# A transformer layer on one core: written out instead of looped, the layer norm's last step on GpSimd, and the first k placed from ACT's queue

## The reference, cut to what matters

```python
def _layernorm(x, axis=-1, eps=1e-05):
    m = jnp.mean(x, axis=axis, keepdims=True)
    v = jnp.var(x, axis=axis, keepdims=True)
    return (x - m) / jnp.sqrt(v + eps)
...
xn = _layernorm(x, axis=-1)
x = x + _L0_attn_ref(xn, ...) + _L0_ffn_ref(xn, ...)
```

## Time and profile before

| | us |
|---|---|
| three runs | 2034.52, 2035.41, 2024.22 |
| their median | 2034.52 |
| the profiled execution | 2030.97 |
| its span, first to last instruction | 2028.7 |

### The profile page before, as it was taken

How to read it: one execution, slowest core, us unless ns; L and a number is a source line. 1 busy time by engine, 2 the same in 40 slices (tenths; PEclk the granted TensorE clock), 3 DMA queues, 4 the chain that set the end, 5 groups by cost and what they waited for, 6 DMA issues and landing times.

```text
span 2028.7 us, 43912 instructions
## 1 busy us (share of the span) xinstructions
PE 1837.6 (91%) x10244; PEld 551.9 (27%) x10244; DVE 1642.4 (81%) x2805; ACT 1441.1 (71%) x3095; POOL 1129.9 (56%) x1695
## 2 busy tenths in 40 slices
PE   4888899999999999999999999999999999999964
PEld 1122222322222232222223232232223223222221
DVE  4999898979889897988989898888989798897110
ACT  1377677877777778777777777777777777777622
POOL 2253538476564837557483755648374664747244
PEclk9999999999999999999999999999999999999978
DMA  3112221212112221212222121222212121220100
GB/s 101 48 52 81 59 76 58 76 55 82 55 56 77 59 77 49 84 55 59 74 59 78 51 82 54 67 67 57 78 57 77 54 70 63 57 76 29 44 24 5
DMA packets 120255, 125.89 MB, mean 62 GB/s; under 512 B 35196, under 2 KB 86780, under 8 KB 119932
## 3 DMA queue, kind: packets, MB, share of 16 engines
q1 hardware_dynamic: 120072, 124.18, 20.2%
HBM read 29.11 MB, written 22.02 MB: 25 GB/s over the span
## 4 chain that ended last, share of the span: by engine, by line
PE 60%; DVE 20%; issue 10%; SPq 4%; ACT 3%; POOL 1%; DMA 1%; DVEq 1%; ACTq 0%; POOLq 0%
PE score_ps L551 16%; PE o_ps L586 15%; DVE negmax L851 14%; PE side_ps L658 12%; PE side_ps L645 6%; PE side_ps L627 3%; SPq L429 2%; SPq L431 2%; PE shift_ps L566 2%; PE side_ps L615 2%; PE side_ps L650 1%; PE side_ps L631 1%; DVE weights L859 1%; ACT weights L694 1%; PE side_ps L640 1%
## 5 line engine op out<-in xcount | busy, mean ns | idle before, releaser
L851 DVE TENSOR_REDUCE negmax<-score_ps 128x1 f32<-128x512 f32 x2048 | 1302.5, 682 | 215.5 <-PE score_ps L551 202.4
L694 ACT ACTIVATE weights<-shift_ps 128x512 f32<-128x512 f32 x2048 | 1120.3, 603 | 328.3 <-PE shift_ps L566 296.4
L551 PE MATMUL score_ps<-kt,qt 48*128 48x512 bf16 x2048 | 678.1, 396 | 94.8 <-DVE negmax L851 78.1
L566 PE MATMUL shift_ps<-qt,kt 51*128 51x512 bf16 x2048 | 671.4, 390 | 2.5 <-ACT weights L694 1.8
L586 PE MATMUL o_ps<-weights,vt 128*32 128x512 f32 x4096 | 556.6, 616 | 0.0
L1048 POOL TENSOR_SCALAR weights<-weights 128x2048 f32<-128x2048 f32 x192 | 364.3, 1897 | 225.9 <-ACT weights L694 213.1
L551 PEld LDWEIGHTS score_ps<-kt,qt 48*128 48x128 bf16 x2048 | 147.1, 94 | 886.6 <-DVE negmax L851 791.2
L658 PE MATMUL side_ps<-w_sb,hidden 128*128 128x512 f32 x512 | 255.2, 621 | 22.5 <-ACT spread L728 14.0
L728 ACT ACTIVATE spread<-side_ps,gate 128x128 f32<-128x128 f32 x512 | 159.5, 372 | 153.5 <-PE side_ps L658 153.5
L566 PEld LDWEIGHTS shift_ps<-qt,kt 51*128 51x128 bf16 x2048 | 152.1, 94 | 50.1 <-ACT weights L694 37.7
L645 PE MATMUL side_ps<-x1T,w_up_sb 128*128 128x512 f32 x256 | 152.4, 679 | 11.3 <-DVE hidden L896 5.6
(11 more groups left out here) (108 smaller groups left out, 1387.7 us busy)
## 6 DMA issues: line engine op xcount, KB each, us to landing
qt<-q_parts SPq DMA_DIRECT2D x768, 32.0 KB
kt<-k_parts SPq DMA_DIRECT2D x768, 32.0 KB
o_rows<-o_sb SPq DMA_DIRECT2D x64, 256.0 KB, 2.0
swung<-turned SPq DMA_DIRECT2D x64, 128.0 KB, 2.4
heads_raw<-o_rows SPq DMA_DIRECT2D x64, 128.0 KB
inv_wide<-inv_rows SPq DMA_DIRECT2D x32, 256.0 KB, 3.2
x_in<-in_x_dram SPq DMA_DIRECT2D x16, 256.0 KB, 2.9
xn_mid<-xn_new SPq DMA_DIRECT2D x16, 256.0 KB, 3.0
```

Source lines behind the costliest of these rows:

```text
L551: pe.matmul(score_ps[:, score_bank(a, t), :], qt[a][row:row + HROWS, slot, 128 * tile:128 * tile + 128], kt[a][row:row + HROWS, slot, :], ...
L566: pe.matmul(shift_ps[:, shift_bank(a, t), :], kt[a][row:row + HROWS + MROWS, slot, 128 * tile:128 * tile + 128], qt[a][row:row + HROWS + M ...
L694: act.activation(weights[:, i % 8, tile, :], shift_ps[:, shift_bank(a, t), :], ACT.Exp, scale=SCALE).then_inc(weighed, 1)
L851: dve.tensor_reduce(negmax[:, i // 8, tile, i % 8:i % 8 + 1], score_ps[:, score_bank(a, t), :], AX.X, ALU.max, negate=True).then_inc(max_t ...
```

## The change

It does four things. All iterations are written out, from -1 to 18. The twelve k transfers of each half of the heads of the first sample's plain attention are issued from ACT's queue, at the end of iteration -1, term by term as the parts of k are done; SyncE issues only q's there. VectorE no longer subtracts the mean and scales: GpSimd does it behind the power, four tiles in a row. And the tables hold other quarters, with GpSimd's lists in another order.

```diff
-EVEN = [("v0", [1]), ("x1T", [3]), ("max_rope1", [5]), ("v1", [9]), ("gates", [12]), ("up0", [13]), ("down0", [18]),
+EVEN = [("v0", [1]), ("x1T", [3]), ("max_rope1", [5]), ("v1", [9]), ("gates", [11]), ("up0", [13]), ("down0", [18]),
...
-ODD = [("xnT", [0]), ("q_plain", [4]), ("k_plain", [8]), ("max_plain1", [11]), ("exp0", [14]), ("exp1", [17]),
-       ("exp2", [21]), ("exp3", [25]), ("exp4", [29]), ("exp6", [33]), ("exp5", [37]), ("y_rope", [40]),
-       ("exp7", [46]), ("max_rope0", [49]), ("q_rope", [53]), ("k_rope", [56])]
+ODD = [("xnT", [0]), ("q_plain", [4]), ("k_plain", [9]), ("max_plain1", [11]), ("exp0", [14]), ("exp1", [17]),
+       ("exp2", [21]), ("exp3", [26]), ("exp4", [29]), ("exp5", [33]), ("exp6", [37]), ("y_rope", [40]),
+       ("exp7", [46]), ("max_rope0", [49]), ("q_rope", [53]), ("k_rope", [57])]
...
-AT = {"merge": 40, "invert": 28, "hi0": 6, "hi1": 7, "mid0": 11, "mid1": 16, "copy1": 18, "copy0": 52, "z": 33,
-      "shares": 34, "top": 25, "square_x1": 44, "scale_x1": 50, "square_out": 7, "scale_out": 15, "stats": 40,
-      "moments": 53, "norm": 59, "act_x1T": 0, "act_max_rope1": 1, "act_up": 1, "act_max_plain0": 1, "act_v": 1,
-      "act_max_plain1": 1, "act_xnT": 1, "act_q_plain": 1, "act_q_plain_2": 3, "act_k_plain": 0,
+AT = {"merge": 40, "invert": 28, "hi0": 8, "hi1": 11, "mid0": 11, "mid1": 18, "copy1": 18, "copy0": 52, "z": 32,
+      "shares": 36, "top": 28, "square_x1": 44, "scale_x1": 53, "square_out": 7, "scale_out": 16, "stats": 40,
+      "moments": 49, "act_x1T": 0, "act_max_rope1": 1, "act_up": 1, "act_max_plain0": 1, "act_v": 1,
+      "act_max_plain1": 0, "act_xnT": 1, "act_q_plain": 1, "act_q_plain_2": 3, "act_k_plain": 0,
...
-            for b in range(-1, FIRST_LOOP):
+            for b in range(-1, B + 3):
                 even(b)
                 odd(b)
                 if b == -1 and after_first:
                     after_first()
-            with eng.Fori(FIRST_LOOP, LAST_LOOP + 1) as b:
-                even(b)
-                odd(b)
-            for b in range(LAST_LOOP + 1, B + 3):
-                even(b)
-                odd(b)
+
+        def place_term(eng, a, gh, t, ab, is_q):
+
+            row, c = HALF * ab + 8 * t, 2 * gh + ab
+            to, parts, part = (qt, q_parts, Q_PART) if is_q else (kt, k_parts, K_PART)
+            eng.dma_start(to[a][row:row + 8, 4 * gh:4 * gh + 4, :],
+                          parts[a][c:128:4, part[t], :]).then_inc(qk_landed[a][gh], 16)
...
                 for t in range(TERMS):
                     for ab in range(2):
-                        row, c = HALF * ab + 8 * t, 2 * gh + ab
-                        sp.dma_start(qt[a][row:row + 8, 4 * gh:4 * gh + 4, :],
-                                     q_parts[a][c:128:4, Q_PART[t], :]).then_inc(qk_landed[a][gh], 16)
-                        sp.dma_start(kt[a][row:row + 8, 4 * gh:4 * gh + 4, :],
-                                     k_parts[a][c:128:4, K_PART[t], :]).then_inc(qk_landed[a][gh], 16)
+                        place_term(sp, a, gh, t, ab, True)
+                        if not (b + lag == 0 and a == PLAIN):
+                            place_term(sp, a, gh, t, ab, False)
...
+                    if t == UNIT - 1 and b == -1:
+                        for gh in range(2):
+                            for term in range(TERMS):
+                                if gh == 0 and term in (0, 2, 5):
+                                    act.wait_ge((hi_done, mid_done, lo_done)[K_PART[term]][PLAIN], 2)
+                                for ab in range(2):
+                                    place_term(act, PLAIN, gh, term, ab, False)
...
-                        if t == AT["norm"] + tile:
-                            if tile == 0:
-                                dve.wait_ge(rstd_done, cnt(b, 1, 1, 1))
-                                need(dve, mid_landed, cnt(b, 1, 16, 0))
-                            dve.tensor_scalar(xn_new[:, tile, :], x_in[:, tile, :], moments[:, tile, 0:1],
-                                              ln_rstd[:, tile:tile + 1], ALU.subtract, ALU.mult).then_inc(xn_done, 1)
...
                     pool.tensor_tensor(ln_rstd[:, :], ln_var[:, :], minus_half[:, :], ALU.pow).then_inc(rstd_done, 1)
+                    pool.wait_ge(rstd_done, cnt(b, 1, 1, 1))
+                    need(pool, mid_landed, cnt(b, 1, 16, 0))
+                    for tile in range(NT):
+                        pool.tensor_scalar(xn_new[:, tile, :], x_in[:, tile, :], moments[:, tile, 0:1],
+                                           ln_rstd[:, tile:tile + 1], ALU.subtract, ALU.mult).then_inc(xn_done, 1)
...
             def even(b):
+                split_max(b, "max_rope1")
                 turn(b, 0)
-                split_max(b, "max_rope1")
+                square_out(b)
                 turn(b, 1)
-                square_out(b)
...
+                third(b, 0, ROPE, 0, q_rest, q_parts)
                 third(b, 0, ROPE, 1, k_rest, k_parts)
-                third(b, 0, ROPE, 0, q_rest, q_parts)
                 split_max(b, "max_plain0")
                 place_v(b, PLAIN)
+                router(b, False)
                 divide(b, PLAIN)
-                router(b, False)
                 spread_of_x(b)
...
-                third(b, 1, PLAIN, 1, k_rest, k_parts)
                 third(b, 1, PLAIN, 0, q_rest, q_parts)
                 mix(b, 0)
+                third(b, 1, PLAIN, 1, k_rest, k_parts)
                 mix(b, 1)
```

More of the change, by code:

```diff
@@ L1205, in odd @@
                 mix(b, 3)
+                mix(b, 4)
                 clip(b, 6)
-                mix(b, 4)
+                clip(b, 8)
                 divide(b, ROPE)
-                clip(b, 8)
                 mix(b, 5)
@@ L1212, in odd @@
                 square_x1(b)
+                clip(b, 9)
+                root(b, -1, 0)
+                place_v(b, ROPE)
                 clip(b, 10)
-                root(b, -1, 0)
-                clip(b, 9)
                 mix(b, 6)
-                place_v(b, ROPE)
                 mix(b, 7)
+                norm_weight(b, x1, 0, -1, x1_done)
                 clip(b, 12)
-                norm_weight(b, x1, 0, -1, x1_done)
                 clip(b, 13)
```

## The result

| | before | after |
|---|---|---|
| median of the runs on one chip, us | 2030.69 (4 runs) | 1976.33 (4 runs) |
| lowest to highest, us | 2024.22 to 2035.41 | 1970.52 to 1979.40 |
| profiled execution, us | 2030.97 | 1978.97 |
| its span, us | 2028.7 | 1977.1 |
| from the rope multiplication of iteration 2 to that of 14, us | 1406.40 | 1363.86 |

The ratio is 0.9731, with a 95% interval of 0.9689 to 0.9773: 54 us faster. The forecast was 1981 us. Its total held, by luck.

What follows compares the result with a forecast made beforehand. TensorE was taken to pace odd steps while expert products run, VectorE the ends of steps. Gains of 30 + 12 + 8.3 + 0.6 = 51 us off the profiled 2030.97 gave about 1980, stated as 1981, range 1964 to 2009.

Steps and rivals of the forecast that it cites:

- no loop: Borders of the looped iterations: without jumps and computed counts, 2.5 us less in each of 12, 30 us (20 to 40).
- norm on GpSimd: Ends of even steps: VectorE loses four instructions, 0.80 us less for each of 15 samples, 12 us (0 to 20).
- tables and GpSimd's order: Shifts of one to three quarters and GpSimd's reordered lists, inside stretches of equal load: costed at 0, within 5 us.
- first k by ACT: Start of the kernel: SyncE issues 12 placements and ACT 12, first score at 28.5 for 36.81: 8.3 us (1.7 if serial).
- the end: Last sums of expert products on GpSimd: the last waits only for exp7's scaled copies, 0.6 us sooner.
- Rival 3: Iteration borders: written-out code comes in slower than a loop, or the stall has another cause; 2011 us, chance 0.08.
- rival 4: Start of odd steps: SyncE's maxima become the bound, so the norm's 12 us go; 1993 us, 0.14 together with rival 1.
- rival 1: GpSimd's and VectorE's SBUF accesses exclude each other, so the norm gives nothing; 1993 us, 0.14 together with rival 4.
- Rival 5: Odd steps' transposes: GpSimd late with normalised rows, slower overall if each takes over 3.2 us; about 2100 at 4 us; chance 0.02.
- Rival 2: First k placements: SyncE's and ACT's queues issue in turn, not at once, first score near 35 us; 1988 us, chance 0.12.

Runs made afterwards that it cites:

- the second kernel: The kernel before with a loop body of two iterations, so 6 passes in place of 12: 2056.8 us, ratio 1.0122.

## Why the prediction was right, by its steps

| step | forecast, us | measured, us |
|---|---|---|
| no loop | 30 (20 to 40) | 25 alone; 30.2 within twelve iterations |
| norm on GpSimd | 12 (0 to 20) | 3 alone, 0 to 3 in the kernel after, 6 once SyncE is not waited for |
| tables and GpSimd's order | 0 (-5 to 5) | 22 alone, 23 undone |
| first k by ACT | 8.3 (1.7 to 8.3) | 5 |
| the end | 0.6 | 0 |
| sum | 51 | 55 by the parts, 54 together |

**No loop: right**, in size and in place. The 2.5 us chosen between 1.81 and 3.31 came out as 2.52, and as 2.2 with the new tables. One reading was off: the prediction has VectorE stop on TensorE's scores at the border, but with the tables alone the score had been ready for 2.06 us, so it is VectorE that is late behind its own jump. Rival 3 fell in its first form, that straight code is slow to come in: 182 fetches of instructions, as many as before, and no stop. It lives in the second kernel, where the loop's body, not its absence, was what had to be fetched.

**The tables: the step that failed.** The prediction costed the shifts of one to three quarters at 0 because they "move work inside stretches where its engine has the same load". They brought 22 us, four times its bound. The load was the wrong thing to compare. What it left out is whether a side product's input or bank is ready when TensorE, which works in order, comes to it. The list of TensorE's waits in the kernel before has such rows, and the prediction did not read it:

```profile
PE side_ps L627 <- DVE q_rest L954: 8.1, 16, 1.4
PE side_ps L627 <- DVE turned L970: 6.9, 10, 1.4
PE side_ps L658 <- ACT max_rows L703: 4.8, 14, 0.8
PE side_ps L608 <- DVE k_rest L954: 0.5, 1, 0.5
```

These waits explain only part: the sum of these four groups falls only from 20.3 to 15.1 us with the tables alone. `q_rest` falls from 8.1 to 1.4 and `max_rows` from 4.8 to nothing, but `k_rest` grows from 0.5 to 6.3. Together with them fell the half-rate stretches, 41 us to none, and the uneven steps. The clock is not the main cause: in iteration 8 of the two written-out kernels with the norm on VectorE, with no half rate in either, the odd step takes 60.9 us with the old tables and 59.9 with the new ones. Which shifts make the rest of the 22 us stays open.

**The norm: rival 4 came true for most of it.** The 0.80 us an even step were measured right, and given back at the start of odd steps while SyncE's 24 placements waited for the residual. The prediction had named that place, and gave it, with rival 1, 0.14. Its argument against it, iteration 15 without idle time, rested on one step of one execution; in the kernel after that same step takes 8.4 us from quarter 60 to quarter 4 of the next, where it took 5.0, and 5.0 again with the residual's load moved. Rival 1 fell: an instruction takes 792 to 809 ns everywhere, at 6.7 us too, where VectorE does nothing. VectorE's clip (L865) did slow, from a mean of 996 to 1101 ns; but it takes 1109 with the new tables and the norm on VectorE, and 1012 with the old ones and the norm on GpSimd. It follows GpSimd's lists more than the quarters: 1083 with the old quarters alone, 1017 with the old lists alone. No loss of time goes with it, since the kernel with the old lists is no faster. The rule of the Trainium skill (Perfetto Trace Analysis, Optimizing Scalar/DVE Operations) gave 39 for the sum by making the norm worthless; it came out nearly worthless, for another reason. Rival 5 had its margin right: done at 959.2, wanted at 963.6.

**First k: the mechanism right, three sizes off.** The first score was forecast at 28.5 and came at 31.66. SyncE starts at 20.68 and not 19.0: 1.7 us, of which 1.4 come from the norm, 0.80 us a tile where 0.45 was taken from the nearest shape. Its last transfer starts at 28.85, so its eleven steps take 0.74 us each and not 0.656, while ACT issues beside it: 1.0 us. And the score follows 2.8 us behind the last, not 2.3. Rival 2 fell: two queues issuing in turn would have doubled the step. ACT's own 24 are issued over the same time and beyond it, 0.65 to 0.78 us apart. The Trainium skill (Perfetto Trace Analysis, DMA Instruction, HWDGE) has the descriptor generator locked by the issuing sequencer. The trace disagrees with the strong reading of it, by which one queue would stand while the other issues; a slowing from 0.656 to 0.74 is all that these rows show. The cover behind ACT held: its copy of v ends at 36.84 and the second v product comes at 38.94.

**The end.** The last scaled copies and the last sum in the timelines of ACT and GpSimd in the kernel after:

```profile
1964.23 1.14 ACT L727 ACTIVATE spread<-side_ps,gate 128x128 f32<-128x128 f32 x4 [2.08 <-PE side_ps L657]
...
1965.50 0.72 POOL L1110 TENSOR_TENSOR two<-spread 128x256 f32<-128x256 f32 x1 [1.42 <-issue]
```

GpSimd's last sum now starts 1.3 us behind the start of ACT's last scaled copies, where it was 1.8, so the 0.5 us are there. The stretch behind the last mark is not shorter all the same. It varies from 269 to 279 us among these kernels, with 53 to 65 us of it at half rate, and 0.6 us cannot be seen in it.

So the total was right by luck, because errors met: 22 us were missed in the tables, and some 10 were too many in the norm, 3 in the start and 5 in the loop.

## What to carry to other kernels

In a kernel whose engines work in order, read the list of waits product by product before a table of places is costed at nothing. Here shifts of a quarter took 0.8 us off an odd step of 60.8. Where work is taken off the engine that paces a stage, look at which queue feeds the next stage and what that queue waits for: here one transfer moved in SyncE's list was worth 10 us, and made the norm's 6 us real. A loop can cost most at its jump: here 1.7 to 2.1 us of the 2.2 to 2.5 it cost an iteration, and more with a longer body.

## What was not expected of the hardware

- A tensor-scalar on GpSimd with two operands of one value a partition takes 0.80 us for 128x128, and 0.34 us on VectorE. The same shape with two tensors takes 0.45 us on GpSimd.
- A loop body of two iterations stopped TensorE for up to 4.25 us at the jump, fetched 3.3 MB of instructions where 2.2 sufficed for straight code, and made the kernel 26 us slower.
- A copy of 256 KB within SBUF, waited for on SyncE, took from 2.4 to 5.4 us from issue to the next transfer in one execution.
- At the loop's jumps VectorE started 1.7 to 2.1 us after its input was ready, with TensorE's granted clock at 1.00; in straight code it was 0.11 us.
- With the same loop and the same work, the old tables had 41 us at 1.2 GHz within twelve iterations and the new ones none.
